# Transposing x in 32x32 blocks on VectorE instead of on TensorE, in a self-attention kernel

## The reference

```python
q, k, v = (split_heads(einsum('bfe,ed->bfd', x, W)) for W in (W_query, W_key, W_value))
scores = einsum('hbqd,hbkd->hbqk', q, k)
attn = softmax(scores, axis=-1)
out = merge_heads(einsum('hbqk,hbkd->hbqd', attn, v)) + einsum('bfe,ed->bfd', x, W_res)
return relu(out)
```

## Time and profile before

| | |
|---|---|
| median of three runs | 1635.06 us (1634.42 to 1636.45) |
| the profiled execution | 1633.92 us |
| its span, first to last instruction | 1632.1 us |
| granted TensorE clock, mean of the span | 0.994 of full |
| busy: PE, PEld, DVE, ACT, POOL | 98%, 94%, 74%, 67%, 57% |
| DMA | 28% of 16 engines, 82 GB/s |

### The profile page before, as it was taken

The page is one execution under the profiler, slowest core; times in us unless marked ns, Lnnn a source line. Parts: engine busy times, 40 slices in busy tenths (PEclk is TensorE's granted clock), DMA queues, the critical chain, the costliest instruction groups (busy, mean ns, idle before and its releaser), DMA issues.

```text
span 1632.1 us, 95535 instructions
## 1 busy us (share of the span) xinstructions
PE 1606.5 (98%) x41984; PEld 1541.2 (94%) x41984; DVE 1200.2 (74%) x1537; ACT 1096.1 (67%) x1794; POOL 932.6 (57%) x1290
## 2 busy tenths in 40 slices
PE   6999999999999999999999999999999999999997
PEld 6999999999999999999999999999999999999996
DVE  4677777777777777777777777777777777777774
ACT  3676666667676766666676767666676767666664
POOL 2555555565655555565656555555656555555655
PEclk9999999999999999999999999999999999999998
DMA  2222222222223222222222232222222222322221
GB/s 59 76 83 89 83 85 84 84 84 84 84 84 88 83 87 84 84 84 84 84 84 86 83 89 83 86 84 84 84 84 84 84 88 82 88 84 84 84 84 54
DMA packets 271797, 135.33 MB, mean 83 GB/s; under 512 B 9312, under 2 KB 271712, under 8 KB 271712
## 3 DMA queue, kind: packets, MB, share of 16 engines
q1 hardware_dynamic: 270336, 134.25, 28.0%
q10 hardware_dynamic: 1376, 0.26, 0.1%
HBM read 67.37 MB, written 67.11 MB: 82 GB/s over the span
## 4 chain that ended last, share of the span: by engine, by line
PE 98%; issue 1%; DVE 0%; ACTq 0%; DMA 0%; ACT 0%; POOLq 0%; POOL 0%; DVEq 0%
PE ps_so L242 17%; PE ps_pt L231 16%; PE ps_so L220 13%; PE ps_qk L196 8%; PE ps_qk L198 8%; PE ps_qk L197 8%; PE ps_vr L209 8%; PE ps_vr L210 7%; PE ps_vr L211 7%; PE ps_x L186 7%; DMA w_raw<-in_L_rec_W_res_dram 0%; ACTq L334 0%; POOLq L39 0%; DVE attn L378 0%; DVE x_lo L351 0%
## 5 line engine op out<-in xcount | busy, mean ns | idle before, releaser
L150 POOL TENSOR_TENSOR y<-attn,vr 128x256 f32<-128x256 f32 x512 | 341.4, 688 | 596.3 <-issue 585.2
L308 ACT COPY probs_t<-ps_pt 128x512 f32<-128x512 f32 x512 | 302.0, 590 | 423.3 <-PE ps_pt L231 423.2
L362 DVE TENSOR_REDUCE row_max<-ps_so 128x16 f32<-128x1024 f32 x256 | 313.5, 1225 | 339.7 <-PE ps_so L242 339.5
L156 POOL TENSOR_SCALAR y<-y 128x512 f32<-128x512 f32 x256 | 380.7, 1487 | 22.4
L292 ACT COPY qk<-ps_qk 128x512 f32<-128x512 f32 x512 | 301.1, 588 | 65.0 <-PE ps_qk L198 13.9
L196 PE MATMUL ps_qk<-x_hi,w_hi 128*128 128x256 f32 x1024 | 332.7, 325 | 5.6 <-DVE x_lo L351 3.3
L231 PE MATMUL ps_pt<-ident,probs 128*128 128x128 f32 x2048 | 323.2, 280 | 0.8 <-ACT probs_t L308 0.7
L300 ACT COPY vr<-ps_vr 128x512 f32<-128x512 f32 x512 | 297.8, 582 | 33.8 <-PE ps_vr L211 1.5
L367 DVE TENSOR_TENSOR shifted<-ps_so,row_max 128x1024 f32<-128x1024 f32 x256 | 313.5, 1225 | 8.8
L209 PE MATMUL ps_vr<-w_hi,x_hi 128*128 128x256 f32 x1024 | 310.8, 304 | 0.1
L242 PE MATMUL ps_so<-vr,probs_t 64*64 64x33 f32 x8192 | 293.0, 222 | 4.2 <-issue 2.8
(11 more groups left out here) (23 smaller groups left out, 2249.0 us busy)
## 6 DMA issues: line engine op xcount, KB each, us to landing
x_in<-in_r_x_dram SPq DMA_DIRECT2D x256, 256.0 KB, 2.8
out_dram<-y SPq DMA_DIRECT2D x256, 256.0 KB, 2.3
w_raw<-in_L_rec_W_query_dram ACTq DMA_DIRECT2D x1, 64.0 KB, 3.1
w_raw<-in_L_rec_W_key_dram ACTq DMA_DIRECT2D x1, 64.0 KB, 3.7
w_raw<-in_L_rec_W_value_dram ACTq DMA_DIRECT2D x2, 32.0 KB, 3.2
w_raw<-in_L_rec_W_res_dram ACTq DMA_DIRECT2D x2, 32.0 KB, 2.5
```

The source lines that it names most:

```text
L150: nc.gpsimd.tensor_tensor(y[:, n % 2, a * HALF:(a + 1) * HALF].rearrange("k t (p j d) -> k j (t p) d", j=2, d=D), attn[:, n % 2, a * HALF: ...
L156: nc.gpsimd.tensor_scalar(y[:, n % 2], y[:, n % 2], 0.0, None, ALU.max).then_inc(y_ready, 1)
L362: nc.vector.reduce_max(row_max[:, :].rearrange("q (h u) -> q h u", h=HEADS), scores, AX_X).then_inc(max_ready, 1)
```

## The change

- **Loading.** x is loaded with 32-token blocks on partitions. For each quarter `b` of the features (32 of them) a DMA of its own fills partitions 32b to 32b+31; partition 32b+t holds, for each of the 16 blocks of 32 tokens in the body, the 32 features of token t of the block. So the body takes four DMAs on SP in place of one, and each piece that lies together in memory is 32 floats (128 bytes) where it was 128 floats (512 bytes).
- **Transposing.** DVE transposes `x_in` into the new SBUF buffer `x_t` in 32x32 blocks, one instruction of 128x512, at the head of `split_x`. It now waits for `x_loaded`. `x_hi` and `x_lo` read `x_t` from SBUF and no longer `ps_x` from PSUM. `transpose_x` and `ps_x` are gone.
- **The free bank** goes to `ps_pt`, which now has two; `transpose_probs` of the two halves run back to back, and ACT copies the two halves back to back.
- **The order on PE** changes: weigh_values of i-2 comes ahead of score of i. The waits for DVE and POOL stand at the end of step i, ahead of the last three matmuls of project_vr, and ask for one step more than they did: `shifted_ready` of body i and `attn_ready` of body i-2, which DVE produces in its own step i.
- **DVE** waits for `o_done` at the reciprocal instead of at the row maximum.

```diff
+    x_blocks = x.rearrange("(n u s) (g t) (b i) -> n b t (u s g) i", u=TILES, s=SEQS, t=BLK, i=BLK)
-        x_in = sb("x_in", [P, 2, TILES, E])
+        x_in = sb("x_in", [P, 2, TOK])
+        x_t = sb("x_t", [P, TOK])
-        ps_x, ps_qk, ps_vr, ps_pt = banks("ps_x"), banks("ps_qk"), banks("ps_vr"), banks("ps_pt")
+        ps_qk, ps_vr, ps_pt = banks("ps_qk"), banks("ps_vr"), banks("ps_pt", 2)
 # SP
-                sp.dma_start(x_in[:, n % 2], x_bodies[i]).then_inc(x_loaded[n % 2], 16)
+                for b in range(E // BLK):
+                    sp.dma_start(x_in[b * BLK:(b + 1) * BLK, n % 2].rearrange("t (c i) -> t c i", i=BLK),
+                                 x_blocks[i, b]).then_inc(x_loaded[n % 2], 16)
 # PE, step
-                if has(i - 1):
-                    pe.wait_ge(shifted_ready, i)
-                if has(i - 3):
-                    pe.wait_ge(attn_ready, i - 2)
-                if has(i - 2):
-                    pe.wait_ge(pt_ready, halves(i - 2, 1))
-                    pe.wait_ge(v_moved, (i - 2) * 2 + 2)
-                if has(i):
-                    pe.wait_ge(qk_ready, halves(i, 1))
-                    score(i)
                 if has(i - 2):
                     weigh_values(i - 2, (n + 2) % RING, 0)
                     weigh_values(i - 2, (n + 2) % RING, 1).then_inc(o_done, 1)
+                if has(i):
+                    pe.wait_ge(qk_ready, halves(i, 1))
+                    score(i)
                 if has(i - 1):
                     pe.wait_ge(probs_ready, i)
                     transpose_probs(i - 1, 0)
+                    transpose_probs(i - 1, 1)
                 if has(i + 1):
                     project_qk(i + 1, (n + 1) % RING, 0)
                 if has(i):
                     project_vr(i, n, 0)
-                if has(i - 1):
-                    transpose_probs(i - 1, 1)
                 if has(i + 1):
                     project_qk(i + 1, (n + 1) % RING, 1)
-                if has(i + 2):
-                    transpose_x(i + 2, n)
-                if has(i):
-                    project_vr(i, n, 1)
+                if has(i):
+                    project_vr(i, n, 1, range(0, 1))
+                if has(i):
+                    pe.wait_ge(shifted_ready, i + 1)
+                if has(i - 2):
+                    pe.wait_ge(attn_ready, i - 1)
+                if has(i - 1):
+                    pe.wait_ge(pt_ready, halves(i - 1, 1))
+                    pe.wait_ge(v_moved, (i - 1) * 2 + 2)
+                if has(i):
+                    project_vr(i, n, 1, range(1, HALF))
 # ACT, step
                 if has(i - 1):
                     copy_pt(i - 1, 0)
+                    copy_pt(i - 1, 1)
...
-                if has(i - 1):
-                    copy_pt(i - 1, 1)
 # DVE, split_x
+                dve.wait_ge(x_loaded[n % 2], dma_count(i, n, 4))
+                if has(i - 1):
+                    dve.wait_ge(xlo_ready, i)
+                nc.vector.transpose(x_t[:, :], x_in[:, n % 2]).then_inc(xt_done, 1)
                 dve.wait_ge(xt_done, i + 1)
-                nc.vector.tensor_copy(x_hi[n][:, :], ps_x[:, :]).then_inc(xhi_ready, 1)
+                nc.vector.tensor_copy(x_hi[n][:, :], x_t[:, :]).then_inc(xhi_ready, 1)
                 dve.wait_ge(xhi_ready, i + 1)
-                nc.vector.tensor_tensor(x_lo[n][:, :], ps_x[:, :], x_hi[n][:, :].bitcast(F32),
+                nc.vector.tensor_tensor(x_lo[n][:, :], x_t[:, :], x_hi[n][:, :].bitcast(F32),
                                         ALU.subtract).then_inc(xlo_ready, 1)
 # DVE, step
                     dve.wait_ge(s_done, i + 1)
-                    if has(i - 2):
-                        dve.wait_ge(o_done, i - 1)
...
                 if has(i - 2):
-                    if not has(i):
-                        dve.wait_ge(o_done, i - 1)
+                    dve.wait_ge(o_done, i - 1)
```

More of the change, by code:

```diff
@@ L15 @@
 F = 64
+BLK = 32
 PAIRS = 2
@@ L34, in attention_program @@
     assert N * SEQS * TILES == B and N % RING == 0 and N > 2 * RING
-    x_bodies = x.rearrange("(n u s) f e -> n (s f) u e", u=TILES, s=SEQS)
+    x_blocks = x.rearrange("(n u s) (g t) (b i) -> n b t (u s g) i", u=TILES, s=SEQS, t=BLK, i=BLK)
     out_bodies = out.rearrange("(n u s) f e -> n (s f) u e", u=TILES, s=SEQS)
@@ L180, in _ @@
         def _(pe):
-            def transpose_x(i, n):
-                pe.wait_ge(x_loaded[n % 2], dma_count(i, n, 1))
-                if has(i - 1):
[L184 to L187, removed]
             def project_qk(i, n, a):
@@ L199, in project_qk, with project_vr @@
                 last.then_inc(qk_done, 1)
-            def project_vr(i, n, a):
-                if a == 1 or has(i - 1):
+            def project_vr(i, n, a, tiles=range(HALF)):
+                if tiles[0] == 0 and (a == 1 or has(i - 1)):
                     pe.wait_ge(vr_ready, halves(i, a) - 1)
@@ L205, in project_vr @@
                 w_vr_lo = w_lo[:, 2:4, :].rearrange("p w c -> p (w c)")
-                for t in range(HALF):
+                for t in tiles:
                     ps = ps_vr[:, t * 2 * COLS:(t + 1) * 2 * COLS]
@@ L211, in project_vr @@
                     last = nc.tensor.matmul(ps, x_lo[n][:, tok], w_vr_hi, start=False, stop=True)
-                last.then_inc(vr_done, 1)
+                if t == HALF - 1:
+                    last.then_inc(vr_done, 1)
             def score(i):
@@ L225, in transpose_probs @@
             def transpose_probs(i, a):
-                if a == 1 or has(i - 1):
-                    pe.wait_ge(pt_ready, halves(i, a) - 1)
+                if has(i - 1):
+                    pe.wait_ge(pt_ready, halves(i - 1, a))
                 for t in range(HALF):
@@ L230, in transpose_probs @@
                         c, pair = t * PAIRS + p, probs[:, a * HALF + t, p * 2:p * 2 + 2, :].rearrange("q j f -> q (j f)")
-                        last = nc.tensor.transpose(ps_pt[:, c * P:(c + 1) * P], pair, ident[:, :])
+                        last = nc.tensor.transpose(ps_pt[:, a * BANK + c * P:a * BANK + (c + 1) * P], pair, ident[:, :])
                 last.then_inc(pt_done, 1)
@@ L248, in step @@
             def step(i, n):
-                if has(i - 1):
-                    pe.wait_ge(shifted_ready, i)
-                if has(i - 3):
-                    pe.wait_ge(attn_ready, i - 2)
                 if has(i - 2):
-                    pe.wait_ge(pt_ready, halves(i - 2, 1))
-                    pe.wait_ge(v_moved, (i - 2) * 2 + 2)
+                    weigh_values(i - 2, (n + 2) % RING, 0)
+                    weigh_values(i - 2, (n + 2) % RING, 1).then_inc(o_done, 1)
                 if has(i):
@@ L258, in step @@
                     score(i)
-                if has(i - 2):
-                    weigh_values(i - 2, (n + 2) % RING, 0)
-                    weigh_values(i - 2, (n + 2) % RING, 1).then_inc(o_done, 1)
                 if has(i - 1):
@@ L282, in _ @@
             project_qk(0, 0, 1)
-            transpose_x(1, 1)
             run_looped(pe, step)
@@ L307, in copy_pt @@
                     act.wait_ge(o_done, i)
-                nc.scalar.copy(probs_t[:, a].rearrange("p c q -> p (c q)"), ps_pt[:, :]).then_inc(pt_ready, 1)
+                nc.scalar.copy(probs_t[:, a].rearrange("p c q -> p (c q)"), ps_pt[:, a * BANK:(a + 1) * BANK]).then_inc(pt_ready, 1)
             def step(i, n):
```

1 line of the change is left out of this document (removed).

## The result

The changed kernel takes 1582.07 us (median of 4 runs, 1581.16 to 1584.35) where the kernel before takes 1634.74 us (median of 4, 1632.23 to 1636.45). The ratio is 0.968, with a 95% interval of 0.966 to 0.970: 52.7 us faster, where 39 were forecast. The profiled execution has a span of 1579.9 us.

A forecast was written before the change was run, and what follows sets the result against it. PE bounds the kernel at 6.224 us a body; afterwards a 6.07 us ring through DVE decides. 256 x (6.224 - 6.07) = 39 us less, 1 us more at the start: 1595.5 us, range 1573 to 1616 (8 in 10: 1573 to 1900).

The forecast's parts named there:

- PE's gain: On PE: losing the x transposes and two restarts saves 0.52 us a step, 133 us if that were all.
- the ring: Score, DVE maximum to attn, wait, last three project_vr matmuls, weigh_values, back to score: 6.07 us a step, setting the pace.
- ACT's stall: PE ahead of the second project_qk waits for ACT's copy of qk: 0.20 us, hidden in the wait for attn.
- End of score to the maximum: From PE going on to the next group until DVE starts the row maximum: 0.21 us.
- the start: Start of the kernel: x_lo's delay was to add about 1 us, once.
- that sign: PE's gaps, about 0.36 us a step, end by DVE attn; forecast wrong if PE waits longest for something else.
- The cover: On PE at the wait for attn: 0.14 us to spare, hiding the stall for ACT's copy.
- PE's own work: PE's step without waits: falls from 6.23 to 5.71 us.
- The rival with the port: DVE and POOL exclude each other for whole instructions at SBUF: 1871 or 2025 us, chance 0.30.
- The full gain of PE: The chain through DVE is shorter than thought, so PE's whole saving of 133 us arrives: 1501 us, chance 0.04.
- ACT's copy: The stall ahead of the second project_qk outgrows its 0.14 cover: step 6.15 to 6.25, 1615 to 1641 us, chance 0.10.
- The small pieces: x's 128-byte DMA pieces bind above 40 ns each; at 50 ns 1909 us, chance 0.04. Forecast cost 12.8 ns each.

The follow-up runs named there:

- e4: Kernel before with only the new loads and the DVE block transpose; PE order, waits and single ps_pt bank as before: 1536.44 us, ratio 0.941.
- e3: Changed kernel with second probability transposes back between first vr half and second qk half, and waits ahead of the very last project_vr matmul: 1536.29 us, ratio 0.941.
- e2: Changed kernel with the waits for DVE and POOL ahead of the very last project_vr matmul instead of the last three: 1572.02 us, ratio 0.963.
- e1: Changed kernel with the second probability transposes and their copy back between first vr half and second qk half, waits kept late: 1580.22 us, ratio 0.968.
- e9: Changed kernel with the waits for DVE and POOL three matmuls earlier, ahead of the whole second half of project_vr: 1679.08 us, ratio 1.029.
- e8: Kernel before with only the loads in 128-byte pieces, four DMAs a body; output not the reference's: 1629.39 us, ratio 0.998.
- e5: Changed kernel with POOL's additions and relu replaced by memsets of y, parts of the output left out: 1579.67 us, ratio 0.967.
- e6: Changed kernel with the DVE block transpose done twice, the first into a buffer nobody reads: 1590.55 us, ratio 0.974.
- e10: e4 with the second probability transposes cut in two around the second project_qk, ACT copying qk first: 1645.17 us, ratio 1.008.

## Why the prediction was right, and where its sizes were off

**The mechanism held.** Of PE's gain most was taken back by a ring that the moved waits close. e4 measures the one (96 us), the kernel after the rest (52), e3 the same gain with a shorter ring and ACT's stall away, and e2, e1 and e9 show that the ring's length is what counts: 0.36 us more gives a step 0.36 longer.

**The ring, term by term**, forecast and then e1's rows, where the ring alone holds PE. End of score to the maximum: 0.21 and 0.11 (0.10 in the kernel after, 804.89 to 804.99). The maximum to attn's end: 3.37 and 3.37. Release: 0.14 and 0.10. The last three matmuls: 0.45 and 0.52. weigh_values and score: 1.90 and 1.91. Sum: 6.07 forecast, 6.01 by the rows, 6.05 as a mean with the fourth steps, of which the forecast knew nothing. The mis-sized term is the first. It was taken from a step in which weigh_values is the last group ahead of the maximum; now score is. e4, with the order of before, has 0.21 again (804.16 to 804.37). That the sum came out within 0.02 of the mean is in part luck: the restart of PE and the fourth step make up for what the first term and the release had too much. Of the 13.4 us between forecast and result the ring accounts for 256 x 0.02 = 5.

**Most of the rest is the start.** I said 1 us more. From maximum to maximum the step before is 6.23 us (the 6.224 of the prediction is a count of bodies in a window, and 1.5 us short in all). Start, end and what lies around the span were 1634.7 - 256 x 6.23 = 40 us before and are 1582 - 256 x 6.05 = 33 now. The start of before holds a stall that nothing in my sum spoke of; e8 loses part of it with the loads alone. What it is stays open.

**The wait that was named wrong.** The prediction said: gap ended by DVE attn, ACT's stall hidden with 0.14 to spare. It also said that it would be wrong on the ring if PE waits longest for something else. PE's only listed wait in the kernel after is for ACT, and yet the ring is there: that sign was a bad one, since of two chains of one length the list names the one that comes first in the step. ACT's stall came near its size (0.20; 0.17 by the waits, 0.13 by starts), by two errors that cancel: the eight transposes ahead of it take 0.84 us (804.89 to 805.73) and not 0.78, and PE goes on 0.06 behind the end of the copy (807.32 to 807.38) and not 0.14. The cover was used up by PE's restart behind the stall (807.38 to 807.60, 0.22 for 0.12), by the longer transposes and by the shorter ring. e1 and e2 were needed to see the tie; a reader who had trusted the list would have removed ACT's stall and got 2 us at most.

**PE's own work** was right where the transposes of the probabilities stand apart: 5.79 us by the terms and 5.79 in e3's undisturbed steps. For the changed kernel the prediction had 5.71, with a second restart saved by making one group of the eight transposes. But the group takes 0.84 us where the two took 0.42 and 0.35 (808.77 to 809.19 and 804.47 to 804.82 in the same trace), which uses up 0.07 of the 0.08; without the stall (0.13) and the restart behind it (0.10) the rows of the kernel after give 6.01 - 0.23 = 5.78. Since the ring was longer than either, this did not touch the forecast.

**DVE.** The transpose takes 701 ns, 0.69 was forecast from equal sizes. `x_hi` takes 0.47 and not 0.69; in e5, with POOL's reads gone, 0.43. The Trainium skill (VectorE: DVE Perf Modes, The perf-mode tier table) has the float32 copy from SBUF at twice the rate; the trace of e5 agrees, 0.26 us less (429 ns for 691 out of PSUM) where the estimate from that page was 0.27. `x_lo` takes 1.06 and not 0.69. The errors cancel in part, and DVE's idle time was 0.45 for a forecast of 0.40.

**The rival with the port** did not come, though its cause is there: e5 shows 0.41 us a step lost to POOL. It was to decide once DVE loses more than its idle time. The loss uses 0.41 of 0.87, since the faster cast and DVE's own overlaps gave it more room than the 0.40 I had counted. The Trainium skill (SBUF — State Buffer, Who interferes with whom) says that such an instruction blocks or is blocked for a whole instruction. Here the trace disagrees: `x_lo` runs from start to end inside relu (e6), at 0.98 us instead of 0.69, and in the kernel after the cast starts 0.03 us behind the transpose (809.02 behind 808.99) and ends at 809.48, while POOL's additions run from 808.51 to 810.02. Had it been held for the whole, e6 would have taken 1864 us and not 1590.55. The measurement decides: the two slow each other down.

**The other rivals.** The full gain of PE needs the ring gone, and e3 and e4 stop at 1536. ACT's copy does not bind alone. The small pieces were costed rightly: the page's 41.2% of 16 engines is 0.412 x 16 x 1579.9 / 256 = 40.7 us of engine time a body, 2.54 us on each, against 0.9 + 1.6; with 27 ns for each of the 512 pieces of y, one of the 2048 of x takes 13.1 ns (12.8 forecast). Four issues on SP hold it for 1.9 us a step (1.5 to 2.6 forecast), and no one waits for them.

## What to carry to other kernels

When a wait is moved so that an engine asks for something of the same step, it closes a ring: add up everything from the producer's input to the wait and from the wait to that input again, and compare it with the engine's own work. Everything queued between the wait and the work that feeds the producer is part of it; e9 and e10 turn a gain of 96 us into a loss by such an order alone. Take work off the binding engine first with order and waits as they are, and measure that. And where a removed stall brings nothing, try it together with the next suspect: two chains of one length show only as a pair, here 2 and 10 us alone and 46 together. A list of waits names one of them; it does not rule out the other.

## What the runs showed of the hardware that I had not expected

- DVE and POOL stretch each other without taking whole turns: a two-input subtraction of 128x512 takes 693 ns beside POOL's fills, 1060 beside its additions and relu, 980 when it lies inside relu; relu takes 1487 (before), 1541 (e6) and 1806 (after).
- Two block transposes of 128x512 back to back start 0.62 us apart, though one lasts 0.70 (e6).
- The maximum starts 0.21 us behind the point at which PE leaves weigh_values (before, e4) and 0.10 to 0.11 behind the one at which it leaves score (after, e1). Why was not tested.
- Every fourth step, the first of each turn of the loop, is 0.14 us longer in the kernel after and in e1, and 0.25 in e9, where the ring binds. PE starts the held matmul that much later behind attn: 0.24 us for 0.10 in e1, 0.34 in e9 (792.14 to 792.48). In e2, where ACT's copy binds and the ring is 0.24 shorter, all steps are equal. In e3 and e4 some steps are 0.09 to 0.17 longer again, one of four in e4 and two in e3. Why is open.
